# Attention scores on one NeuronCore: three passes over 64 rows of the array, or two passes over 128 rows on operands stacked by DMA, with the projections moved to even slots

## The reference, cut to what matters

```
x = x + attn_a(layernorm(x))
x = x + ffn(layernorm(x))            # top 2 of 8 experts
x = x + attn_b(layernorm(x))         # the stage of this change
x = x + ffn(layernorm(x))

# attn_b, for each of 8 sequences b of 512 tokens and each of 16 heads h
q = Q_h x ; k = K_h x ; v = V_h x    # 64 values per head
att = causal(q k^T / 64) ; p = softmax(att)
z  = sum over heads of W_h (p v)
```

## Time and profile before

| | |
|---|---|
| median of 3 runs | 1552.91 us (1551.44 to 1554.37) |
| profiled execution, its own time | 1549.28 us |
| its span | 1547.5 us |
| busy share of the span: PE, PEld, DVE, ACT, POOL | 85%, 73%, 72%, 61%, 49% |
| mean granted TensorE clock over the span | 0.915 |
| span of the long attention's head scores | 444.5 to 1283.2 us |

### The profile page before, as it was taken

One profiled execution on the slowest core, in us unless ns is written; L12 is line 12 of the kernel. 1 busy time (PEld: TensorE's weight loads), 2 busy tenths in 40 slices (PEclk: granted clock), 3 DMA queues, 4 the chain that ended last, 5 costly groups with the idle time before them and its releaser, 6 DMA issues. The chain is left out here.

```text
span 1547.5 us, 28434 instructions
## 1 busy us (share of the span) xinstructions
PE 1320.2 (85%) x8377; PEld 1124.9 (73%) x8377; DVE 1109.0 (72%) x2822; ACT 951.5 (61%) x2522; POOL 765.4 (49%) x954
## 2 busy tenths in 40 slices
PE   2687635999759999999999999999999996499990
PEld 1576625888748888888888888888888884388880
DVE  5665444777638788888887888888888874377771
ACT  1554313444338878888788788787888884144440
POOL 3005562444415565576575665765755755244443
PEclk9877657999959999999999999999999996599995
DMA  9391011222100000000000000000000000122215
GB/s 182 122 364 33 30 40 48 57 57 56 31 28 15 1 15 1 1 25 5 3 25 3 17 12 1 22 8 1 11 5 5 11 1 14 39 57 56 56 44 163
DMA packets 91936, 64.47 MB, mean 42 GB/s; under 512 B 34020, under 2 KB 77935, under 8 KB 91792
## 3 DMA queue, kind: packets, MB, share of 16 engines
q1 hardware_dynamic: 83152, 45.75, 11.0%
q0 software_dynamic: 8640, 16.93, 3.5%
HBM read 26.59 MB, written 36.96 MB: 41 GB/s over the span
## 5 line engine op out<-in xcount | busy, mean ns | idle before, releaser
L1360 POOL TENSOR_TENSOR b_probs<-b_probs,b_recip 128x128 f32<-128x128 f32 (+3 forms) x512 | 352.7, 719 | 309.0 <-DVE b_recip L1593 309.0
L420 DVE TENSOR_TENSOR b_pt_lo<-b_ring,b_pt_hi 128x512 fp32r<-128x512 f32 (+1 forms) x384 | 218.9, 598 | 93.1 <-ACT b_pt_hi L414 87.8
L545 ACT ACTIVATE b_probs<-b_s_bank,b_neg_max 128x256 f32<-128x256 f32 (+3 forms) x512 | 267.9, 533 | 27.7 <-DVE b_neg_max L537 26.3
L537 DVE TENSOR_REDUCE b_neg_max<-b_s_bank 128x1 f32<-128x256 f32 (+3 forms) x512 | 219.6, 478 | 49.3 <-PE b_s_bank L529 48.3
L1220 POOL DMA_INDIRECT y_rows<-f_y_sb,f_dest x142 | 139.1, 979 | 215.4 <-DVE f_y_sb L1198 208.1
L414 ACT ACTIVATE b_pt_hi<-b_ring 128x512 fp32r<-128x512 f32 (+1 forms) x384 | 192.3, 547 | 9.1 <-PE b_ring L485 8.4
L81 PE MATMUL b_s_bank<-b_k_hi,b_q_hi 64*128 64x256 f32 (+3 forms) x512 | 181.2, 354 | 2.9 <-ACT b_probs L545 1.4
L485 PE MATMUL b_ring<-ident,b_probs 128*128 128x128 f32 x1280 | 179.4, 278 | 4.7 <-DVE b_q_lo L420 4.7
L82 PE MATMUL b_s_bank<-b_k_lo,b_q_hi 64*128 64x256 f32 (+3 forms) x512 | 164.9, 322 | 0.0
L83 PE MATMUL b_s_bank<-b_k_hi,b_q_lo 64*128 64x256 f32 (+3 forms) x512 | 164.2, 321 | 0.0
L554 PE MATMUL b_pv_bank<-b_pt_hi,b_v 128*128 128x512 f32 (+3 forms) x512 | 158.8, 322 | 6.0 <-DVE b_y L1556 4.9
(11 more groups left out here) (303 smaller groups left out, 3348.5 us busy)
## 6 DMA issues: line engine op xcount, KB each, us to landing
x_sorted<-a_blank SPq DMA_DIRECT2D x64, 260.0 KB, 3.8
f_xs<-x_sorted SPq DMA_DIRECT2D x142, 65.0 KB
b_yc<-y_rows SPq DMA_DIRECT2D x16, 256.0 KB, 3.1
f_yc<-y_rows SPq DMA_DIRECT2D x16, 256.0 KB, 3.2
y_rows<-f_y_sb,f_dest POOLq DMA_INDIRECT x142
x_tok<-in_L_attn_a_x_dram SPq DMA_DIRECT2D x8, 256.0 KB, 4.9
out_dram<-x_tok SPq DMA_DIRECT2D x8, 256.0 KB, 2.4
f_raw<-in_L_ffn_W_dram SPq DMA_DIRECT2D x1, 1408.0 KB, 6.8
```

Source lines behind the costliest of these rows:

```text
L420: nc.vector.tensor_tensor(dst, src(rg.of(key)), hi.bitcast(F32), ALU.subtract).then_inc(rg.lo_done, 1)
L537: nc.vector.tensor_reduce(sc.neg_max[:, i:i + 1], s_tile(sc, i), AX.X, ALU.max, negate=True).then_inc(sc.max_done, 1)
L545: nc.scalar.activation(probs[:, P_AT[i]:P_AT[i] + (i + 1) * P], s_tile(sc, i), ACT.Exp, bias=sc.neg_max[:, i:i + 1], accum_out=sums[:, i:i ...
L1360: nc.gpsimd.tensor_tensor(part, part, recip[:, i:i + 1].to_broadcast([P, (i + 1) * P]), ALU.mult).then_inc(probs_done, 1)
```

## The change

Three things change in `attention_b`.

First, the scores. The parts of q and k lie in one tensor `qk` in the order q_hi, k_hi, k_lo, q_lo. For each head SyncE copies 64 partitions of it into a tensor `stack[u % 2]` of 128 partitions by three DMAs: q_hi, k_hi, k_lo to partitions 0 to 63 (64 rows of 6 KB), q_lo to partitions 64 to 127 of the first third (64 rows of 2 KB), and k_hi, k_lo to partitions 64 to 127 of the other two (64 rows of 4 KB); 768 KB for a head. A score tile is then two passes of contraction 128, with [q_hi; q_lo] stationary against [k_hi; k_hi] and [k_lo; k_lo]. This adds the term lo·lo.

Second, the projection of a pair goes from odd to even slots, and one slot earlier: pair p is projected in slot 2p-2, where it was slot 2p-1. The list of slots begins at -2. ScalarE's and VectorE's splits of q and k move with it, and wait until both heads of the previous pair have been stacked.

Third, some buffers share their place: `xn` lies in `yc[1]`, the router's `xn_t` in `z`, its `over` in `apart`; the loads of `yc` come later and in between the stacking DMAs on SyncE's queue.

```diff
-    slots = range(-1, NU + NH)
+    slots = range(-2, NU + NH)
     def paired(u):
-        return (u + 1) // 2 if u % 2 and 0 <= u + 1 < NU else None
+        return u // 2 + 1 if u % 2 == 0 and 0 <= u + 2 < NU else None
...
-        q = (sb("q_hi", [P, T], F32R), sb("q_lo", [P, T], F32R))
-        k = (sb("k_hi", [P, T], F32R), sb("k_lo", [P, T], F32R))
+        qk = sb("qk", [P, 4, T], F32R)
+        q, k = (qk[:, 0, :], qk[:, 3, :]), (qk[:, 1, :], qk[:, 2, :])
+        stack = [sb(f"stack{i}", [P, 3, T], F32R) for i in range(2)]
+        stack_in = [sem(f"stack_in{i}") for i in range(2)]
...
         @block.sync
         def _(sp):
-            for b in range(NB):
+            def rows_of(b):
                 wait(sp, yc_added, b)
+                if b:
+                    ring_filled(sp, rg, ("xn", b - 1))
...
+            def stacked(u):
+                pair, half = divmod(u, 2)
+                rows = qk[half * KD:half * KD + KD].bitcast(F32)
+                to = stack[half][:].bitcast(F32)
+                sp.wait_ge(rg.lo_done, rg.lo["k", pair])
+                wait(sp, sc.s_full, (u - 1) * len(S_GROUPS))
+                sp.dma_start(to[0:KD, :, :], rows[:, 0:3, :]).then_inc(stack_in[half], 16)
+                sp.dma_start(to[KD:P, 0, :], rows[:, 3, :]).then_inc(stack_in[half], 16)
+                sp.dma_start(to[KD:P, 1:3, :], rows[:, 1:3, :]).then_inc(stack_in[half], 16)
+
+            rows_of(0)
+            for u in range(NU):
+                stacked(u)
+                if u == 0:
+                    rows_of(1)
+                b, h = divmod(u, NH)
+                if h == NH // 2 and b + 2 < NB:
+                    rows_of(b + 2)
...
             def scores(u, group):
-                if u % 2 == 0 and group == 0:
-                    pe.wait_ge(rg.lo_done, rg.lo["k", u // 2])
-                rows = slice(u % 2 * KD, u % 2 * KD + KD)
+                if group == 0:
+                    pe.wait_ge(stack_in[u % 2], (u // 2 + 1) * 3 * 16)
                 s_free(pe, sc, u, group)
                 for i in S_GROUPS[group]:
-                    st = [part[rows, i * P:i * P + P] for part in q]
-                    mv = [part[rows, 0:(i + 1) * P] for part in k]
-                    three_passes(nc, s_tile(sc, i), st, mv, i == S_GROUPS[group][0], False)
+                    for part in (1, 2):
+                        nc.tensor.matmul(s_tile(sc, i), stack[u % 2][:, 0, i * P:i * P + P],
+                                         stack[u % 2][:, part, 0:(i + 1) * P],
+                                         start=(i == S_GROUPS[group][0] and part == 1), stop=False)
...
                 if paired(u) is not None:
-                    split_hi(nc, act, rg, ("q", paired(u)), q[0][:])
-                    split_hi(nc, act, rg, ("k", paired(u)), k[0][:])
+                    for copied in stack_in:
+                        wait(act, copied, paired(u) * 3 * 16)
+                    split_hi(nc, act, rg, ("q", paired(u)), q[0])
+                    split_hi(nc, act, rg, ("k", paired(u)), k[0])
```

More of the change, by code:

```diff
@@ L571, with __init__ @@
 class Route:
-    def __init__(self, nc, ctx, name, buffers, pl):
+    def __init__(self, nc, ctx, name, buffers, pl, xn_t=None):
         sb = lambda n, s, d: ctx.enter_context(nc.sbuf_tensor(f"{name}_{n}", s, d))
@@ L580, in __init__ @@
         self.scattered = pl.scattered
-        self.xn_t = sb("xn_t", [P, T], F32)
+        self.xn_t = sb("xn_t", [P, T], F32) if xn_t is None else xn_t
         self.scores = sb("scores", [P, QT * NE], F32)
@@ L601, in __init__ @@
         self.count = sb("count", [P, NE], F32)
-        self.over = sb("over", [P, NE, CAP // P], F32)
+        self.over = self.apart[:].rearrange("p (k e) j -> p k (e j)", k=NE)
         self.tiles = sb("tiles", [P, NE], F32)
@@ L765, in plan_tiles @@
     dve.wait_ge(pl.step, 2)
-    nc.vector.tensor_tensor(pl.over[:], per(pl.count[:]), g.steps[:].unsqueeze(1).to_broadcast([P, NE, CAP // P]),
+    nc.vector.tensor_tensor(pl.over, per(pl.count[:]), g.steps[:].unsqueeze(1).to_broadcast([P, NE, CAP // P]),
                             ALU.is_gt).then_inc(pl.step, 1)
     dve.wait_ge(pl.step, 3)
-    nc.vector.tensor_reduce(pl.tiles[:], pl.over[:], AX.X, ALU.add).then_inc(pl.step, 1)
+    nc.vector.tensor_reduce(pl.tiles[:], pl.over, AX.X, ALU.add).then_inc(pl.step, 1)
     dve.wait_ge(pl.step, 4)
@@ L1284, in attention_b @@
         rg = Ring(nc, ctx, "b_ring", 3, order)
-        rt = Route(nc, ctx, "b_r", 1, pl)
+        z = sb("z", [P, T], F32)
+        rt = Route(nc, ctx, "b_r", 1, pl, z)
         n = Moments(nc, ctx, "b_n")
@@ L1289, in attention_b @@
         xn_hi, xn_lo = sb("xn_hi", [P, 2 * T], F32R), sb("xn_lo", [P, 2 * T], F32R)
-        xn = sb("xn", [P, T], F32)
         yc = [sb(f"yc{k}", [P, QT, D], F32) for k in range(NK)]
+        xn = yc[1][:].rearrange("p t d -> p (t d)")
         probs = [sb(f"probs{i}", [P, NPT], F32) for i in range(2)]
@@ L1298, in attention_b @@
         y_parts = (sb("y_hi", [P, T], F32R), sb("y_lo", [P, T], F32R))
-        z = sb("z", [P, T], F32)
-        q = (sb("q_hi", [P, T], F32R), sb("q_lo", [P, T], F32R))
-        k = (sb("k_hi", [P, T], F32R), sb("k_lo", [P, T], F32R))
+        qk = sb("qk", [P, 4, T], F32R)
+        q, k = (qk[:, 0, :], qk[:, 3, :]), (qk[:, 1, :], qk[:, 2, :])
+        stack = [sb(f"stack{i}", [P, 3, T], F32R) for i in range(2)]
+        stack_in = [sem(f"stack_in{i}") for i in range(2)]
         yc_in = sem("yc_in")
@@ L1577, in _ @@
                 if paired(u) is not None:
-                    split_lo(nc, dve, rg, ("q", paired(u)), q[1][:], q[0][:])
-                    split_lo(nc, dve, rg, ("k", paired(u)), k[1][:], k[0][:])
+                    for copied in stack_in:
+                        wait(dve, copied, paired(u) * 3 * 16)
+                    split_lo(nc, dve, rg, ("q", paired(u)), q[1], q[0])
+                    split_lo(nc, dve, rg, ("k", paired(u)), k[1], k[0])
                 if coming(u, TURNED) is not None:
```

## The result

The changed kernel takes **1530.66 us** (median of 4 runs, 1529.92 to 1532.25), against 1552.18 us of the kernel before on the same chip (4 runs, 1548.40 to 1554.37): a ratio of 0.9874, 95% interval [0.9858, 0.9889], some 20 us faster. The forecast was 1510 and its own range 1485 to 1532; the direction was right, the gain a little less than half of the 43 us forecast.

A forecast was written before the change was run, and what follows sets the result against it. TensorE was taken to set the pace at 6.59 us a head. Removing 0.82 and losing 0.445 to waits nets 0.375 a head, 48 us; less 5 at the start, 43 us faster: 1510 us, range 1485 to 1532.

The forecast's parts named there:

- change of width 64 to 128 rows: TensorE's scores: 0.10 us at the first pass plus 0.08 at the masks go, 0.18 us a head.
- one pass of each tile less: TensorE's scores: one pass of each of four tiles goes, together 0.64 us a head, counted as gain.
- projections in even slots: TensorE waits ahead of the transposes, 1.29 us or 0.49 us in even heads, a loss of 0.445 us a head.
- stacking transfers: Three DMAs a head, 768 KB, landing in 4.8 to 7.2 us, taken as hidden except at the start.
- start of the stage: First stacking, with nothing to hide it, makes the first scores about 5 us later, once.
- my chain: Projection, ScalarE's splits and exponentials, VectorE's reciprocal, GpSimd's scalings, transposes: 7.77 us against 6.48 us of TensorE work.
- rival C: More waits than counted, ScalarE late in even slots, VectorE piling up in odd ones: 1532 to 1556 us, chance 0.18.
- A: The forecast itself: the gain half eaten by the projection's chain, 1485 to 1532 us, chance 0.50.
- my ends: Stacking bandwidth: 311 KB/us as for loads, or 156 KB/us if half the partitions give half the rate.
- the limit of 187 KB/us: Stacking rate from which downward the pair's loop of copying and splitting q and k decides, at 12.4 us a pair.
- D: Stacking DMAs are the bound, with waits for the stack ahead of splits and scores: slower, 1609 us, chance 0.17.
- B: The projection's chain is hidden and TensorE stays the bound: 1453 us, with some waits to 1485, chance 0.15.

The follow-up runs named there:

- x4: Changed kernel with projections in odd slots, three score passes over 128 rows, stacking left out after head 1: 1524.49 us, 0.9827 of the kernel before.
- x3: Changed kernel with projections back in odd slots, two score passes, stacking left out after head 1: 1500.29 us, 0.9661 of the kernel before.
- x1: Changed kernel with only heads 0 and 1 stacked, later heads reading those stacks: 1524.99 us, 0.9826 of the kernel before.
- x2: Kernel before with projections moved to even slots, q and k in two buffers, no stacking, three passes over 64 rows: 1581.73 us, ratio 1.0192.
- x6: Changed kernel with ScalarE's high parts of q and k behind the exponentials of the first banks: 1542.19 us, 0.9972 of the kernel before.
- x9: Changed kernel with everything behind the products one slot later, y in two buffers, other buffers sharing places: 1520.88 us, 0.9838 of the kernel before.
- x7: Changed kernel with three stacks and the shared buffers of x9, projections still in even slots: 1523.40 us, 0.9851 of the kernel before.
- x5: Changed kernel with three stacks, shared buffers of x9, pair p projected in odd slot 2p-3: 1522.52 us, 0.9845 of the kernel before.
- x10: As x3, but a single score pass for each tile: 1489.65 us, 0.9644 of the kernel before.
- x11: As x3, but VectorE splits only 8 of 512 columns of q_lo and k_lo: 1485.75 us, 0.9610 of the kernel before.
- x13: x9 with stacking left out after head 1: 1513.57 us, 0.9791 of the kernel before.
- x14: x9 with the stacking transfers cut to an eighth of their bytes from head 2 on: 1513.74 us, 0.9792 of the kernel before.

## Where the prediction failed, and where it held

In us a head, from the mean of the stage; the rows of the sum are the prediction's own. The steps are taken in this order: the width comes first, while TensorE is still the bound, so what it gives and what the pass gives behind it depend on the order.

| step | forecast | measured | from |
|---|---|---|---|
| change of width 64 to 128 rows | -0.18 | -0.247 | before to x4 |
| one pass of each tile less | -0.64 | -0.178 | x4 to x3 |
| projections in even slots | +0.445 | +0.187 | x3 to x1 |
| stacking transfers | 0 | +0.068 | x1 to the changed kernel |
| sum | -0.375 | -0.170 | |
| start of the stage | +5 us in all | +5.8 us at the first scores | last low part to first scores, both traces |

**What bounds the kernel** was read rightly for the kernel before: TensorE at 99%, and of the first 0.27 us that it gave up (the width) 0.247 came out. My -0.18 for the width came near it partly by luck: 0.08 of it was right, the 0.10 at the first pass was not (0.02), and the 0.17 at the transposes ahead were missing.

**The step that failed** is the term of the dropped pass: 0.64 us a head counted in full, where x4 to x3 give 0.178. I had written "What TensorE gives up counts until another engine or a chain of waits takes over", and used it with only one such chain in mind, the projection's. The second step that failed is that chain: I took GpSimd ahead of L485 for the new wait, and there is none. The removal was real: scores and masks fell to 1.57 us, and TensorE's busy time by 99 us. But the curve over 3, 2 and 1 passes shows that at 6.1 to 6.3 us a head TensorE no longer sets the pace, in odd slots too, where my chain does not exist: VectorE and ScalarE reach 89%, and TensorE waits at the products for VectorE. I had the number for it in hand: I wrote that both engines would be at 88%, and put it into rival C as a risk, instead of asking at which pace the unevenness of single slots stops them. They stopped at 89%.

**Luck in the sum.** The result lies inside the forecast's own range because errors of opposite sign met: the pass was 0.46 us a head too good, the move 0.26 too bad. By the prediction's own signs of being wrong, idle time of TensorE at `b_pv_bank` instead of L485 stands for C and against A; so the mechanism that was forecast is refuted, though its range held.

**The move** costs what it was said to cost in kind, but less than I counted and elsewhere: 0.187 and not 0.445, at the products for VectorE's add into `y`, and not at L485 for GpSimd. The chain that I followed is there: in the slot shown it would have held the transposes by 913.12 - 912.40 = 0.72 us. But the products stand ahead of them in TensorE's order and had already waited 1.26 us, which hides it. What I left out is the far end of ScalarE's queue, the last high parts of the transposed tiles and the lower half of y, and VectorE's add, which comes after both. x2 shows the move alone at +0.26, a loss with nothing against it; x6 shows that the order at the head of ScalarE's queue is not simply wrong: putting the exponentials first costs 0.108 more.

**The transfers** were rightly taken as hidden within 0.07 us, and the bandwidth lies between my ends as far as can be estimated. In the middle of the stage the DMA engines are busy 0.57 at 132 GB/s, before the change 0.04 at 11: the added 121 GB/s for an added share of 0.53 make, as an estimate, 228 GB/s when fully busy, above the limit of 187 KB/us that I had worked out and far below the 311 of the loads. The page "SBUF — State Buffer" of the Trainium skill, in the part on the DMA port swizzle, gives 196 GB/s for 1 MiB on 64 partitions and an asymptote of about 218; the estimate is 16% above the first and 5% above the second. No run here copies over 128 partitions, so none shows how far below the full rate of such a copy this is. That the loop of a pair is a bound close by was right as well: it turns in 12.9 us in x9. What I did not see is its consequence. In even slots, where a pair takes 12.7 to 12.8 us, the stacking is cheap; in odd slots, where the engines could do 12.3 us a pair, its bytes cost up to 0.195 us a head. So the two costs hide one another: taking away the move alone (x7 to x5) or the transfers alone (changed kernel to x1) gives 0.00 and 0.068, both together 0.255 (changed kernel to x3).

**The rivals.** The waits stand where rival C put them, and the size lies at the edge between A and C (1532). D did not happen: the waits for `b_stack` are 11.7 us of ScalarE in the window, 15 times, and a single one of 0.3 us ahead of the scores. B did not either, as even x10 with half the remaining passes stays at 1490. That the clock would keep its level in the middle of the stage held (1.00).

**What stays open.** Which one dependency ends the gain at 6.1 us a head was not isolated. A lighter VectorE gives 0.085, one pass less 0.043; ScalarE's load was not varied, and it is the one that is busiest then (179.44 of 200 us in x11). Why the even phase still costs 0.135 a head after the chain of y was moved (x13 against x3) is open too.

## What to carry to other kernels

Here, with the busiest engine at 99% and two others at 83%, removed work counted nearly in full only for the first few per cent: of the first 0.27 us of a head of 6.57 us 0.25 came out, and the next 0.64 us gave 0.18. Before forecasting, ask at which pace the next engines reach the share at which single slots stop them (here 86 to 89%), and let that be the forecast and not a rival.

A step that is moved must be followed to the last instruction behind it in each queue. The costly ones here were the last splits and a copy at the end of ScalarE's slot, and VectorE's add behind them, one slot away from the projection that was moved.

Two costs can hide one another, so undo them together as well as singly: the move and the transfers looked like 0.19 and 0.07 us, and the version without the move found the transfers at 0.16 to 0.20.

## What was unexpected in the hardware

Going between 64 and 128 rows of the array costs 0.25 to 0.31 us of a head, once there and once back, as much as one more pass of a 512 tile (0.24). It shows at two places, the last transposes ahead (0.74 against 0.57 us) and the masks behind (0.32 against 0.24), and hardly at the first pass (0.22 against 0.20).

Copies within SBUF with 64 partitions on both sides moved 132 GB/s at a busy share of 0.57, by the estimate above about 228 GB/s for busy DMA engines. Transfers of 128, 256 and 384 KB, issued together, all landed 4.8 to 5.0 us after their issue (medians), and their count did not matter: with an eighth of the bytes and as many transfers, the time was that of no transfers (6.274 and 6.275 us a head). The third issue of a head occupied SyncE's queue for 1.6 us in the median in x9 (0.6 to 2.3), where the first took 0.46; with an eighth of the bytes (x14) it took 0.60.
